# Two fused attention layers on one core: a ring of score banks, later transposes, and another order of ScalarE's and VectorE's work in a step

## The reference

```python
x = x + _layernorm(_L0_attn_ref(_layernorm(x), wq, wk, wv, wo))      # 16 heads of 64, causal
x = x + _layernorm(_L0_ffn_ref(_layernorm(x), ...))                  # 8 experts, top 2, gelu
x = x + _layernorm(_L1_attn_ref(_layernorm(x), qkv, wo))             # 16 heads of 8, rotary, causal
x = x + _layernorm(_L1_ffn_ref(_layernorm(x), ...))                  # ternary weights, relu squared
```

```python
scores = jnp.einsum('bhqd,bhkd->bhqk', q, k) * scale
scores = jnp.where(causal, scores, -jnp.inf)
probs = jax.nn.softmax(scores, axis=-1)
out = jnp.einsum('bhqk,bhkd->bhqd', probs, v)
```

## Time and profile before

| what | value |
|---|---|
| median of 3 runs | 1357.96 us (1356.5 to 1360.73) |
| the profiled execution | 1357.62 us |
| its span, first to last instruction | 1355.8 us |
| PE busy | 1155.7 us (85%) |
| DVE busy | 936.2 us (69%) |
| ACT busy | 857.9 us (63%) |
| mean granted TensorE clock | 0.960 |
| layer 0's attention (40.5 to 649) | 608.5 us |
| layer 1's attention (887 to 1293) | 406 us |

### The profile page before, as it was taken

The page is one execution under the profiler, slowest core; times in us unless marked ns, Lnnn a source line. Parts: engine busy times, 40 slices in busy tenths (PEclk is TensorE's granted clock), DMA queues, the critical chain, the costliest instruction groups (busy, mean ns, idle before and its releaser), DMA issues.

```text
span 1355.8 us, 28730 instructions
## 1 busy us (share of the span) xinstructions
PE 1155.7 (85%) x10458; PEld 855.0 (63%) x10458; DVE 936.2 (69%) x2353; ACT 857.9 (63%) x1996; POOL 122.8 (9%) x105
## 2 busy tenths in 40 slices
PE   3698999989898999989989995278888888888886
PEld 2476767757576766758966773145656655655664
DVE  4566666667566666656443337769999999989963
ACT  2466665667566666656034431468999989989933
POOL 1600000000000000000310004200000000000033
PEclk9899999999999999999979997769999999989999
DMA  4311222221212222220010000332022022020001
GB/s 119 83 37 49 53 65 67 64 69 39 70 44 59 54 63 69 64 63 17 17 36 16 15 12 1 106 58 26 12 36 34 5 37 37 2 36 2 2 1 31
DMA packets 29672, 56.77 MB, mean 42 GB/s; under 512 B 4538, under 2 KB 14674, under 8 KB 29410
## 3 DMA queue, kind: packets, MB, share of 16 engines
q1 hardware_dynamic: 28738, 53.43, 17.3%
q10 hardware_dynamic: 800, 1.57, 0.4%
HBM read 25.49 MB, written 4.33 MB: 22 GB/s over the span
## 4 chain that ended last, share of the span: by engine, by line
PE 53%; DVE 21%; issue 14%; ACT 8%; DMA 2%; POOL 1%; SPq 1%; ACTq 0%; DVEq 0%; POOLq 0%
PE pO L1008 12%; PE pT L1067 11%; DVE Zb L761 9%; PE pS L1043 9%; ACT probs L558 4%; PE pT L970 4%; PE pS L1129 4%; PE pT L1141 3%; DVE Sm L775 3%; PE pS L1090 2%; PE pT L974 2%; PE pS L1226 1%; PE pS L1047 1%; PE pS L1206 1%; PE pO L1141 1%
## 5 line engine op out<-in xcount | busy, mean ns | idle before, releaser
L1067 PE MATMUL pT<-cst,probs 128*128 128x128 f32 x2304 | 368.3, 287 | 54.3 <-ACT probs L558 53.0
L540 ACT COPY PT<-pT 128x512 f32<-128x512 f32 (+3 forms) x597 | 275.9, 484 | 102.3 <-PE pT L1067 98.1
L1067 PEld LDWEIGHTS pT<-cst,probs 128*128 128x128 f32 x2304 | 249.2, 143 | 142.3 <-ACT probs L558 98.7
L558 ACT ACTIVATE probs<-pS,nmax 128x128 f32<-128x128 f32 (+7 forms) x256 | 190.5, 744 | 83.2 <-DVE nmax L771 64.6
L1008 PE MATMUL pO<-PT,V 128*64 128x128 f32 (+1 forms) x4608 | 230.9, 277 | 6.2 <-DVE attnT L730 5.6
L771 DVE TENSOR_REDUCE nmax<-pS 128x1 f32<-128x128 f32 (+7 forms) x256 | 192.1, 750 | 52.6 <-PE pS L1047 50.2
L558 ACT ACTIVATE probs<-Sm,nmax 128x128 f32<-128x128 f32 (+7 forms) x256 | 199.3, 778 | 29.2 <-DVE nmax L775 22.7
L761 DVE TENSOR_SCALAR Zb<-pS 128x128 bf16<-128x128 f32 (+7 forms) x256 | 192.8, 753 | 21.1 <-PE pS L1047 20.9
L1043 PE MATMUL pS<-Kh,Qs 128*128 128x512 f32 (+2 forms) x384 | 165.9, 436 | 45.5 <-ACT probs L558 37.6
L1008 PEld LDWEIGHTS pO<-PT,V 128*64 128x64 f32 (+1 forms) x4608 | 180.0, 113 | 26.5 <-DVE attnT L730 9.7
L775 DVE CUSTOM_DVE_ANT_0 Sm<-pS,Zb 128x128 f32<-128x128 f32 (+7 forms) x256 | 193.4, 755 | 4.5
(11 more groups left out here) (177 smaller groups left out, 1271.0 us busy)
## 6 DMA issues: line engine op xcount, KB each, us to landing
Qs<-Ql SPq DMA_DIRECT2D x32, 256.0 KB, 3.5
Kh<-Kh SPq DMA_DIRECT2D x32, 256.0 KB, 3.5
Kl<-Kl SPq DMA_DIRECT2D x32, 256.0 KB, 4.6
wq_t<-factors SPq DMA_DIRECT2D x32, 256.0 KB, 3.9
QS<-split SPq DMA_DIRECT2D x72, 64.0 KB
KS<-split SPq DMA_DIRECT2D x72, 64.0 KB
w0s<-in_w SPq DMA_DIRECT2D x8, 192.0 KB, 3.7
split<-parts SPq DMA_DIRECT2D x2, 768.0 KB, 3.5
```

The costliest lines, as they stand in the source:

```text
L540: nc.scalar.copy(PT[:, g % 2, h, k0 * P:(k0 + nk) * P], pT[r % TBANKS][:, 0:nk * P])\
L558: nc.scalar.activation(probs[:, i % NPROB, 0:n], src[:, 0:n], ACT.Exp, bias=nmax[:, i % 4:i % 4 + 1], scale=sign, accum_out=total).then_in ...
L1067: m = nc.tensor.transpose(pT[r % TBANKS][:, kt * P:(kt + 1) * P], probs[:, item % NPROB, (k0 + kt) * P:(k0 + kt + 1) * P], ident)
```

## The change

- **Ring of score banks.** `pS` becomes one tensor of four banks. An item with qt below 4 takes one bank, a longer one two adjacent banks, in turn (`place_scores`). The scores of item i wait for the last item that used these banks, `after[i]`, which is two to four items back. Layer 1 gets the same.
- **Layer 0's lag.** The transposes of an item come three steps after its scores, where it was two (`lag`); product with V and output one step later too (`queued`, 5 for 4); four `probs` buffers for three. Layer 1 keeps lag 2, queue 4 and three buffers.
- **ACT's order in layer 0.** The exponential of step i ahead of the copies of step i.
- **DVE's order.** In layer 0 DVE's share of a Q or K part is done one step later, after that step's maximum and ahead of its transpose copies (`order_for_dve`), and the counts for it are made anew.
- Buffers in SBUF are moved to make room.

```diff
-    def __init__(self, heads, turns, copies, project):
+    def __init__(self, heads, turns, copies, project, lag):
+        self.lag, self.queued, self.nprob = lag, lag + 2, lag + 1
...
+        self.place_scores()
...
-            if 2 <= step < self.n + 2:
-                c, b, qt, h = self.items[step - 2]
+            if lag <= step < self.n + lag:
+                c, b, qt, h = self.items[step - lag]
...
+    def order_for_dve(self):
+        count = sum("dve" in copies for _, _, copies in self.rounds[:self.ahead])
+        self.dve_at, late = [], []
+        for step, here in enumerate(self.at_step):
+            mine = [r for r in here if "dve" in self.rounds[r][2]]
+            now = late + [r for r in mine if self.rounds[r][0] == "T"]
+            late = [r for r in mine if self.rounds[r][0] == "P"]
+            for r in now:
+                count += 1
+                self.rounds[r][2]["dve"] = count
+            self.dve_at.append(now)
+            self.done_by[step]["dve"] = count
+
+    def place_scores(self):
+        self.bank_of, self.after, last, at = [], [], [-1] * 4, 0
+        for i, (_, _, qt, _) in enumerate(self.items):
+            size = -(-(qt + 1) * P // BANK)
+            at = 0 if at + size > 4 else at
+            self.bank_of.append(at)
+            self.after.append(max(last[at:at + size]))
+            last[at:at + size] = [i] * size
+            at = (at + size) % 4
...
-        pS = [ctx.enter_context(nc.psum_tensor(f"pS{i}", [P, 2 * BANK], F32)) for i in range(2)]
+        pS = ctx.enter_context(nc.psum_tensor("pS", [P, 4 * BANK], F32))
...
-        L = [Attention(HPC, CH0, ["act", "dve"], True), Attention(HPG, G1, ["act"], False)]
+        L = [Attention(HPC, CH0, ["act", "dve"], True, 3), Attention(HPG, G1, ["act"], False, 2)]
...
+                for i in range(plan.n + plan.queued + 1):
+                    if k == 1 and plan.ends_group(i - plan.queued):
+                        factors_out(a, plan.group(i - plan.queued))
+                    if k == 0:
+                        exponential(i)
+                        rounds_out(i)
+                    else:
+                        rounds_out(i)
+                        exponential(i)
...
-                        if i >= 2:
-                            pe.wait_ge(a["p"] if k == 0 else a["mx"], i - 1)
+                        if plan.after[i] >= 0:
+                            pe.wait_ge(a["p"] if k == 0 else a["mx"], plan.after[i] + 1)
...
-                    for r in plan.at_step[i]:
+                    for r in plan.dve_at[i]:
```

More of the change, by code:

```diff
@@ L105, in __init__ @@
         for step in range(self.n + 8):
-            if 2 <= step < self.n + 2:
-                c, b, qt, h = self.items[step - 2]
+            if lag <= step < self.n + lag:
+                c, b, qt, h = self.items[step - lag]
                 for k0 in range(0, qt + 1, TPB):
-                    self.add(step, "T", (step - 2, k0, min(TPB, qt + 1 - k0)), [copies[len(self.rounds) % len(copies)]])
-                self.round_of[step - 2] = len(self.rounds) - 1
+                    self.add(step, "T", (step - lag, k0, min(TPB, qt + 1 - k0)), [copies[len(self.rounds) % len(copies)]])
+                self.round_of[step - lag] = len(self.rounds) - 1
             if project:
@@ L117, in __init__, with scores @@
             self.done_by.append(dict(self.copied))
+        self.order_for_dve()
+    def order_for_dve(self):
[19 more added lines that the diff above has]
+            at = (at + size) % 4
+    def scores(self, pS, i, k0, nk):
+        start = self.bank_of[i] * BANK + k0
+        return pS[:, start:start + nk]
     def project(self, step, c, b, u):
@@ L210, in build @@
         parts = at(136, "parts", [P, 2, PARTS, S], BF16)
+        rdb = at(128, "rdb", [P, 2, P])
+        rs = at(129, "rs", [P, 2, P])
+        probs1 = at(136, "probs1", [P, 3, S])
         xn = at(148, "xn", [P, NT, D])
@@ L524, in attention, with rounds_out @@
                 PT = PT0 if k == 0 else PT1
-                for i in range(plan.n + QUEUED + 1):
-                    if k == 1 and plan.ends_group(i - QUEUED):
-                        factors_out(a, plan.group(i - QUEUED))
+                def rounds_out(i):
                     for r in plan.at_step[i]:
@@ L541, in attention, with exponential @@
                             .then_inc(a["cp_act"], 1)
+                def exponential(i):
                     if i < plan.n:
@@ L760, in mask @@
                         dve.wait_ge(a["p"], i - NMASK + 1)
-                    nc.vector.tensor_scalar(Zb[:, i % NMASK, 0:n], pS[i % 2][:, 0:n], 0.0, MASKED,
+                    nc.vector.tensor_scalar(Zb[:, i % NMASK, 0:n], plan.scores(pS, i, 0, n), 0.0, MASKED,
                                             ALU.is_equal, ALU.mult).then_inc(a["z"], 1)
@@ L774, in maximum @@
                         dve.wait_ge(a["z"], i + 1)
-                        nc.vector.tensor_tensor_reduce(Sm[:, i % NMASK, 0:n], pS[i % 2][:, 0:n], Zb[:, i % NMASK, 0:n],
+                        nc.vector.tensor_tensor_reduce(Sm[:, i % NMASK, 0:n], plan.scores(pS, i, 0, n), Zb[:, i % NMASK, 0:n],
                                                        -(DH1 ** -0.5), 3e38, ALU.add, ALU.min,
                                                        nmax[:, i % 4:i % 4 + 1]).then_inc(a["mx"], 1)
-                for i in range(plan.n + QUEUED + 2):
-                    finished = plan.ends_group(i - QUEUED - 1)
+                for i in range(plan.n + plan.queued + 2):
+                    finished = plan.ends_group(i - plan.queued - 1)
                     summed = k == 1 and plan.ends_group(i - 2)
@@ L785, in attention @@
                     if finished:
[L786 removed]
+                        outputs(plan.group(i - plan.queued - 1))
                     if summed:
@@ L997, in values @@
                     nc.tensor.transpose(pO[:, P:2 * P], rdb[:, g % 2, :], ident)
-                for e2, done in plan.done_by[i - QUEUED + 2].items():
+                for e2, done in plan.done_by[i - plan.queued + plan.lag].items():
                     if done:
```

42 lines of the change are left out of this document (20 added, 22 removed).

## The result

The changed kernel takes **1348.89 us** in the median of 4 runs (1346.51 to 1350.69), the kernel before beside it 1358.33 (4 runs, 1356.5 to 1360.73). The ratio is 0.9938 with a 95% interval of 0.9913 to 0.9963: faster, by more than the 0.3% that can be told from nothing, and by 9.4 us where 23 were forecast. The profiled execution has a span of 1344.7 us for 1355.8. Of these 11.1 us layer 0's attention gives 9.6, layer 1's 1.1 (404.9 for 406.0), all the rest 0.4.

What follows compares the result with a forecast made beforehand. Engines waiting for one another in layer 0's attention were taken as the bound, losing 9.4 us a turn. The terms summed as 1357.6 - 37 + 16 - 2 = 1334.6, given as 1335; range 1305 to 1358, likeliest case 1326 to 1348.

Steps and rivals of the forecast that it cites:

- What bounds the kernel: Layer 0's attention: engines wait for one another; PE's work is 66.4 us a turn, and a turn loses 9.4.
- Steps 0 to 12: First half of a layer 0 turn: loss falls from 9.4 to 4.7 us, 8 turns, -37.
- Steps 20 to 31: Second half of a layer 0 turn: later rests and transfers cost 2.3 us a turn, 7 turns, +16.
- The K transfers: End of a layer 0 turn: no slack, 4.9 to 5.4 us to land, the scores wait 0.75 us more.
- The ring: Score banks: priced at nothing in layer 0, -2 us in layer 1 (ends 0 and -10).
- Steps 12 to 19: Long items of a layer 0 turn: nothing, covered by the product with V; without that cover about 1 us a step.
- the lag's end: End of layer 0: one more step of draining over short items, nothing to +1 us.
- only changes its name: Rival: stall passes from exponential to bank, first half losing 7, second 2.5; 1354 to 1357 us; no change 0.09.
- The slower rival: Steps 22 to 31: late rests hold `pT` banks, PE stops; slower above 5.6 us a turn; 1364 us, chance 0.10.

Runs made afterwards that it cites:

- e2: The changed kernel with ACT's copies ahead of its exponential again in all steps of layer 0; 1344.33 us, ratio 0.9917.
- e8: The changed kernel with the exponential first only in steps 16 to 31 of a turn, copies first in steps 0 to 15; 1334.94 us, ratio 0.9824.
- e4: The changed kernel without the ring, score banks as two fixed buffers of two again in both layers; 1352.77 us, ratio 0.9966.
- e12: e10 with the first half's parts in steps 2, 4, ... 12 in place of 1, 3, ... 11; 1307.97 us, ratio 0.9638.
- e17: e12 with transpose copies of steps 2, 4, 6, 8 on DVE and of steps 3, 5, 7, 9 on ACT; 1305.18 us, ratio 0.9634.
- e3: The changed kernel with layer 0 back at lag 2, queue 4 and three probs buffers; 1347.68 us, ratio 0.9927.
- e9: The changed kernel with copies first throughout layer 0 and DVE's rests of Q and K parts late only in steps 0 to 15; 1364.42 us, ratio 1.0055.
- e10: e9 with lag 2 and queue 4: the kernel before plus the ring and rests late in first halves only; 1325.9 us, ratio 0.9781.
- e5: The kernel before with one edit, ACT's exponential ahead of its copies in layer 0; 1435.56 us, ratio 1.0561.
- e15: The kernel before with one part of the change, the ring of score banks in both layers; 1347.45 us, ratio 0.9913.

## Why the prediction was wrong in size

- **What bounds the kernel.** Right: 9.2 us lost in a first half (9.4 forecast), 0.2 in a second, PE's work 66.4. Only that three of eight first halves took 1.5 more had no place in it; the changed kernel has these three too, and one in its first turn, so this cost the forecast some 1.5 us in all. But not all of the 9.4 was idle time of PE, and that is the next point.
- **Steps 0 to 12, "the first half loses 4.7 where it lost 9.4 ... 8 turns, -37": the step that failed.** A first half loses 6.3 now, 2.9 less than before, not 4.7, in 7 turns; in the first turn, whose half was 37.8 before and has about 2 us less work in it after, nothing is gained, a stretch at the lower clock (0.68 between 50 and 55) included. That is 20 us in place of 37 (8 x 4.7 is 37.6). PE's busy time in the first half of turn 6, before and after, shows where it failed (stretch, its length, PE busy, granted clock, DMA share, GB/s):

```profile
422.06:461.54 39.48, 33.69 (x271) 1.00 0.23 60
417.41:453.03 35.62, 31.89 (x252) 1.00 0.26 66
```

Before, PE was without work for 5.8 us, and for 3.4 more it was busy beyond the 30.3 that the prices make; after, for 3.7 and 2.6. The stalls that I had laid out are there and rather smaller: 1.75, 0.92 (0.70 and 0.22) and 0.89 for 1.9, 1.2 and 1.1, together 3.6 for 4.2. What I had wrong is the rest. I took the whole 9.4 off, with the part in which PE is busy but its pieces take longer than in a dense stretch, and put back for that part the restarts of three stalls, "4.2, with restarts of 0.14 each about 4.7", so 0.5. It measured 2.6, for 3.4 before. (By the other split of the halves it is 1.9 for 2.7, and the dense second halves have 0.8 of it as well, so a part of it is that the prices are low.) In the chain of work one sees it at the pieces that come after a wait:

```profile
419.22 1.13 PE pT L1017 x2
...
438.55 1.11 PE pT L1021 x8
```

The prices were 0.86 and 0.89. The exponential's side belongs here too, though not as an error of the sum, for the layout had the part's copies behind the exponential: that side is worth 1.4 us a first half by e2 and e8, so in the changed kernel this piece, which I had taken for the source of the gain, lowers it.
- **Steps 20 to 31, +2.3 in 7 turns.** 38.7 for 36.3 is +2.4, but of it 1.0 is the work that lag 3 moves into this half (and out of the first), and 1.4 stalls, 10 us in 7 turns. The layout had 1.2 at the three banks and 0.75 at the transfers, which didn't come; the moved work, which wasn't in the sum, took the place of these. A right number by luck, then, with the banks about right. That it isn't larger is the exponential's doing (e2: 3.35 in its place), which I had not said.
- **The K transfers, 0.75.** Not seen. They landed 4.2 to 4.7 us after issue, at most 4.9 in any turn, not 4.9 to 5.4 as in the earlier trace rows; over the whole of either kernel the median is 4.6, so these rows were of a slow turn. From the end of the rest to the first scores 6.9 us sufficed for 7.3. The rule of the Trainium skill ("DMA: Bandwidth & Descriptors", Anatomy of one DMA), an estimate of 2.6 us for such a transfer, also led to no wait; but the time to landing that it would give isn't what the trace shows.
- **The ring, nothing in layer 0, -2 in layer 1.** Right beside the other edits (e4: nothing; layer 1's attention has a mean of 405.5 in 12 traces with the ring and 408.0 in 5 without, single traces lie between 402 and 410 with it and between 406 and 410 without, so the size is uncertain by about 1). But "the exponential first makes it worth nothing" was a cost of that edit that I took for a property of the ring: with copies first it gives 1.2 alone and 2.3 beside late rests.
- **Steps 12 to 19 nothing; the lag's end 0 to 1.** One small wait, 0.3 us, at the second round of step 18, the round that I had named as closest. Start and end of layer 0 cost 1.3, and the last half 1.7 with no parts in it, 1.1 of which is a product moved into it.

The sum for layer 0's attention, by terms of the trace: -20.3 of losses in first halves (with the stretches at the lower clock in them, three before and four after), +9.8 in second ones, -1.0 of work that lag 3 takes out of the sixteen halves, +0.6 in the last half and +1.3 at the ends, -9.6 in the trace; the forecast had -37 and +16. Nearest of the rivals was that the stall "only changes its name": it had first halves losing 7 and second ones 2.5, the run has 6.3 and 1.6. The slower rival had the right place, but it needed 5.6 us a turn, and there are 1.4 of stalls, or 2.4 with the moved work.

**What stays open**: why e12 still loses 3.3 us a first half (its waits are for exponentials, but moving ACT's copies away in e17 did not shorten it), how the loss of 1.6 in the changed kernel's second halves is divided among its banks, and why PE's pieces in first halves take 2.6 us more than their prices. Rests late with lag 3, parts in steps 2 to 12 and 19 to 29 were not tried together.

## What to carry to other kernels

Before engines' orders are exchanged, look at what shares a step: if two long pieces that recur every second step fall on the same steps, moving one of them by one step can be worth more than any buffer (one constant: 2.6%). When an operation is put first on its engine, price what it is now in front of; if that is a link of the loop that holds a buffer, the gain is only the difference. And compare like with like: where the loss before is taken as the time less the price of the work, and the loss after as a sum of stalls laid out by hand, the time in which an engine is busy but slower than its price (here 3.4 us of 9.4 before, 2.6 of 6.3 after) is forecast away.

## What the runs showed of the hardware that I had not expected

After some stalls PE runs at a lower granted clock. In the changed kernel, around the stall of step 5, the columns of the earlier trace rows:

```profile
200.00:205.00 5.00, 3.25 (x8) 1.77 (x7) 2.39 (x6) 2.68 (x8) 0.00 (x0) 0.70 0.41 105
275.00:280.00 5.00, 3.25 (x19) 2.10 (x21) 2.56 (x8) 3.19 (x9) 0.00 (x0) 1.00 0.26 52
```

and the timeline of the first of these turns:

```profile
199.55 0.61 PE L1114 MATMUL pT<-cst,probs 128*128 128x128 f32 x4
...
201.91 0.41 PE L1114 MATMUL pT<-cst,probs 128*128 128x128 f32 x1 [1.75 <-DVE Ql L756]
...
202.14 2.07 PE L1017 MATMUL pT<-xnT,w0s 128*128 128x512 f32 x2
```

After 1.75 us of idling the part's two matmuls took 2.07 us for 1.02 to 1.10: PE's lower level, 1.2 for 2.4 GHz, and 0.70 is the mean of both over the stretch. In the turn at 275 the same 1.75 us of idling left the clock at 1.00. That is the difference between halves of 35.6 and 37.1, and of 39.5 and 41.1 before. It is also that between 36.5 and 38.1 in e3, where six of eight first halves have it. From 60 us on, no half has it in e2, e8, e9, e10 and e12 to e17. The longest stall doesn't tell which kernels have it: between 60 and 590 PE's waits are at most 1.1 us long in e3, which has the most but for e5, and up to 1.5 and 1.6 in e15, which has none. What decides isn't shown. For whoever compares halves it means that the clock of each has to be read first: with and without such a stretch the same half differs by 1.5 us, as much as most edits here give or cost.

Stages that no edit touched moved too: the 237.5 us between the two attentions were up to 242.5 in other profiles, and 21 runs of the kernel before in one session lie between 1350.8 and 1363.5. Differences of one or two us between kernels are therefore read from the halves, those at full clock, and not from the medians.
